# A decoder layer on one core: half of the last row's state sum moved to TensorE, the last x1 block kept on chip, the second norm by half rows

## What is computed

```
x1  = layernorm(x + attention(x))              # over the 4 rows at each position, causal, 16 heads of 32
u   = silu(conv4(in_proj(ctx)))                # 512 channels per row
h_t = exp(delta_t * A) * h_(t-1) + delta_t * u_t * B_t     # 16 states n per channel
y   = sum_n h[n] * C[n] + D * u
x2  = layernorm(x1 + y * silu(x1))             # "second norm"
out = layernorm(x2 + (silu(x2 Wg) * (x2 Wu)) Wd)
```

## Time and profile before

| | us |
|---|---|
| median of 3 runs | 1078.03 |
| lowest and highest | 1074.52, 1078.8 |
| the profiled execution: its own time | 1081.42 |
| the profiled execution: its span | 1079.6 |
| VectorE busy | 790.4 |
| TensorE busy | 856.6 |
| ScalarE, GpSimd busy | 697.5, 575.0 |

### The profile page before, as it was taken

The page is one execution under the profiler, slowest core; times in us unless marked ns, Lnnn a source line. Parts: engine busy times, 40 slices in busy tenths (PEclk is TensorE's granted clock), DMA queues, the critical chain, the costliest instruction groups (busy, mean ns, idle before and its releaser), DMA issues. The chain is left out here.

```text
span 1079.6 us, 12506 instructions
## 1 busy us (share of the span) xinstructions
PE 856.6 (79%) x3752; PEld 625.1 (58%) x3752; DVE 790.4 (73%) x1262; ACT 697.5 (65%) x1087; POOL 575.0 (53%) x561
## 2 busy tenths in 40 slices
PE   6868798687785978867652657779899999989997
PEld 2536654375443754455331445558777777778886
DVE  3587898877988679873872585699999999545543
ACT  3387995689757897584690464477777787333331
POOL 0049966897679976698695233145545455200000
PEclk8887877788887978888675787789999999999999
DMA  7146989689986898779799761111112111122321
GB/s 242 31 122 147 217 175 214 131 230 236 208 195 123 232 236 201 146 136 248 158 233 246 238 202 58 50 40 50 39 39 58 39 41 36 39 83 66 115 77 50
DMA packets 53686, 146.49 MB, mean 136 GB/s; under 512 B 5684, under 2 KB 14004, under 8 KB 43908
## 3 DMA queue, kind: packets, MB, share of 16 engines
q0 software_dynamic: 9216, 67.11, 32.5%
q1 hardware_dynamic: 43056, 78.53, 21.7%
q10 hardware_dynamic: 1364, 0.25, 0.1%
HBM read 58.97 MB, written 91.10 MB: 139 GB/s over the span
## 5 line engine op out<-in xcount | busy, mean ns | idle before, releaser
L1309 POOL TENSOR_TENSOR state<-state,crep 128x512 f32<-128x512 f32 x256 | 347.8, 1538 | 103.7 <-DVE state L1066 103.6
L1066 DVE TENSOR_TENSOR_SCAN state<-decay,banks 128x512 f32<-128x512 f32 x256 | 294.8, 1202 | 74.7 <-PE banks L566 49.6
L612 PE MATMUL banks<-x2T,wgu 128*128 128x512 f32 x1056 | 250.3, 399 | 28.8 <-POOL wgu L1401 27.3
L566 PE MATMUL banks<-ident,scaled 128*128 128x128 f32 x1024 | 182.1, 324 | 106.6 <-DVE state L1066 91.9
L612 PEld LDWEIGHTS banks<-x2T,wgu 128*128 128x128 f32 x1056 | 202.4, 193 | 75.7 <-issue 27.4
L566 PEld LDWEIGHTS banks<-ident,scaled 128*128 128x128 f32 x1024 | 139.0, 165 | 175.5 <-DVE state L1066 96.2
L788 ACT ACTIVATE decay<-delta,negA 128x512 f32<-128x512 f32 x256 | 170.8, 717 | 98.6 <-DVE state L1066 98.2
L777 ACT ACTIVATE scaled<-duT,BT 128x512 f32<-128x512 f32 x256 | 163.5, 716 | 9.9 <-DVE duT L1043 9.8
L892 ACT ACTIVATE leaf<-bit,table,table_gap 128x512 f32<-128x512 int32 x198 | 149.6, 806 | 20.4 <-DVE w L1095 20.4
L1095 DVE COPY_PREDICATED leaf<-bits,leaf 128x512 f32<-128x512 int32 x132 | 118.8, 914 | 8.0 <-issue 6.9
L1095 DVE COPY_PREDICATED w<-bits,leaf 128x512 f32<-128x512 int32 x99 | 90.1, 910 | 3.3 <-ACT leaf L892 1.7
(11 more groups left out here) (122 smaller groups left out, 1154.5 us busy)
## 6 DMA issues: line engine op xcount, KB each, us to landing
y_scratch<-state POOLq DMA_DIRECT2D x60, 1024.0 KB, 8.7
crep<-c_scratch SPq DMA_DIRECT2D x64, 256.0 KB, 5.3
idx_sb<-in_idx SPq DMA_DIRECT2D x33, 256.0 KB, 2.8
xT_sb<-in_xT SPq DMA_DIRECT2D x16, 256.0 KB, 4.6
x_sb<-in_x SPq DMA_DIRECT2D x4, 1024.0 KB, 19.0
y_scratch<-u SPq DMA_DIRECT2D x4, 1024.0 KB, 6.1
y_scratch<-state SPq DMA_DIRECT2D x4, 1024.0 KB, 6.1
x_scratch<-x_sb SPq DMA_DIRECT2D x4, 1024.0 KB, 8.8
```

Source lines behind the costliest of these rows:

```text
L566: last = nc.tensor.transpose(banks[:, k % NB, lc * LQ:(lc + 1) * LQ], scaled[:, g % SR, lc, et * P:(et + 1) * P], ident[:])
L612: last = mm(banks[:, 2 * tb + w, :], wgu[:, par, w, ws, t * P:(t + 1) * P], x2T[:, tb, xs, t, :], start=t == 0 and n == 0, stop=t == HT - ...
L1066: V.tensor_tensor_scan(state[:, g % GR, et, :], decay[:, k % DR_RING, :], banks[:, k % NB, :], 0.0, ALU.mult, ALU.add).then_inc(scan_ready, 1)
L1309: G.tensor_tensor(state[:, g % GR, et, :], state[:, g % GR, et, :], crep[:, g % CR, :], ALU.mult)\
```

## The change

1. For the last 8 of row 3's 16 states (`G0` = 56 of 64 groups) no DMA adds the products. TensorE adds them: one product with the identity for each unit (`state_summed`), three groups behind the transposes, into the four PSUM banks that are free after the projection; then y of the first eight states, loaded back, is added the same way (`rest_summed`), and `gate_y(3)` reads PSUM. `add_odd_sum(3)` moves up to (11, 3).
2. The last block's x goes into the buffer `conv_in` instead of `x_sb`, with its load moved from row 3's n = 5 to row 2's n = 13. Its x1 stays there and is neither stored nor loaded: `load_row` takes three quarters of x1, `x1_tile` takes the last quarter from the chip.
3. The row loads begin at n = 8 instead of 12. All four gates silu(x1) go to SBUF, in two instructions each. GpSimd multiplies rows 1 and 2 by them in one instruction each, VectorE row 0 in one and row 3 in four.
4. The second norm goes by eight half rows k, with two banks each, woven with parts of `select`.
5. The convolution taps of rows 1 to 3 move from (1, 0)...(1, 3) to (1, 2), (1, 3), (2, 0), (2, 1).

The core of the diff, with less indentation; where a function's body is new only its new lines are shown:

```diff
+sb("conv_at", [P, 72])
+conv_in = sb("conv_in", [P, ET, L])
...
+gate_in = ctx.enter_context(nc.sbuf_tensor("gate_in", [P, 2, ROW], f32))
...
+x_last = conv_in
+x_at = lambda c: x_sb if c < S - 1 else x_last
...
+G0 = DS * S - DS // 2
...
+    if g >= G0:
+        return ysum_out, ET * (g - G0) + ET
     if g % DS == 1:
...
+yb = [t[:, 0:ROW].rearrange("p (t l) -> p t l", l=L) for t in taken]
+x1b = [t[:, ROW:2 * ROW].rearrange("p (t h) -> p t h", h=H) for t in taken]
+gate = [gate_in[:, 0, :], gate_in[:, 1, :], gate_in[:, 0, :], flat_h[:, 2 * ROW:3 * ROW]]
+gate = [t.rearrange("p (t h) -> p t h", h=H) for t in gate]
+ON_POOL = {1: 1, 2: 2}
+GATED = {0: 1, 3: 5}
+row_gated = lambda b: (pool_gated, ON_POOL[b]) if b in ON_POOL else (gated, GATED[b])
+def x1_tile(b, lt):
+    return x1b[b][:, lt, :] if lt < 3 else x_last[:, b, :]
...
+HALVES = [(b, (2 * h, 2 * h + 1)) for b in range(S) for h in range(2)]
+def half_bank(k, i):
+    return 2 * (k % 4) + i
...
-            if c:
+            if c == S - 1:
+                sp.wait_ge(delta_ready, ET * S)
+                sp.wait_ge(x_in, 16 * c)
+            elif c:
                 sp.wait_ge(x1_out, 16 * c)
-            sp.dma_start(x_sb[:], x.rearrange("s (c p) h -> p s c h", p=P)[:, :, c, :]).then_inc(x_in, 16)
+            sp.dma_start(x_at(c)[:], x.rearrange("s (c p) h -> p s c h", p=P)[:, :, c, :]).then_inc(x_in, 16)
...
-            sp.dma_start(x1b[b], x1_scratch[b].rearrange("(t p) h -> p t h", p=P)).then_inc(x1_in[b], 16)
+            sp.dma_start(x1b[b][:, 0:3, :], x1_scratch[b].rearrange("(t p) h -> p t h", p=P)[:, 0:3, :])\
+                .then_inc(x1_in[b], 16)
             sp.dma_start(yb[b], y_scratch[b].rearrange("(p t) l -> p t l", p=P)).then_inc(y_in[b], 16)
...
-                if n == 5 and b:
+                if n == 5 and 0 < b < S - 1:
                     load_x(b)
+                if n == 13 and b == S - 2:
+                    load_x(b + 1)
...
-                if b == S - 1 and n == 10:
-                    store_x1(b)
-                if b == S - 1 and n == 12:
-                    sp.wait_ge(x1_out, 16 * S)
+                if b == S - 1 and n == 8:
+                    sp.wait_ge(shift_ready, S)
+                    sp.wait_ge(x1_out, 16 * (S - 1))
+                if b == S - 1 and 8 <= n < 8 + S - 1:
+                    load_row(n - 8)
+                if b == S - 1 and n == 11:
                     sp.dma_start(table[:], lut.to_broadcast([P, 16])).then_inc(lut_in, 16)
-                    load_idx(0, 0)
-                if b == S - 1 and n >= 12 and n - 12 < S - 1:
-                    load_row(n - 12)
-        load_idx(0, 1)
-        load_idx(0, 2)
+                    for c in range(3):
+                        load_idx(0, c)
+        sp.wait_ge(decay_ready, UNITS)
+        sp.wait_ge(scaled_ready, S * DS * S)
+        load_row(S - 1)
         store_x2(0)
         next_idx(0, 0)
-        load_row(S - 1)
         store_x2(1)
...
+        def state_summed(g, et):
+            if g == G0 and et == 0:
+                pe.wait_ge(res_ready, S * S)
+                pe.wait_ge(attT_ready, S * S)
+            pe.wait_ge(hc_ready, ET * g + et + 1)
+            mm(banks[:, NB + et, :], ident[:], state[:, g % GR, et, :], start=g == G0, stop=False)\
+                .then_inc(ysum_out, 1)
+        def rest_summed():
+            pe.wait_ge(y_in[S - 1], 16)
+            for et in range(ET):
+                mm(banks[:, NB + et, :], ident[:], yb[S - 1][:, et, :], start=False, stop=True)\
+                    .then_inc(ysum_out, 1)
         pe.wait_ge(ip_in, 16)
         pe.wait_ge(ident_in, 16)
...
+        def residual(k):
+            b, lts = HALVES[k]
+            if k < 2:
+                pe.wait_ge(scan_ready, UNITS)
+            elif k < 4:
+                pe.wait_ge(gated, GATED[S - 1])
+            else:
+                pe.wait_ge(x2lo_ready, 2 * (k - 4) + 2)
+            pe.wait_ge(*row_gated(b))
+            for i, lt in enumerate(lts):
+                if i + k == 0:
+                    pe.wait_ge(x1_ready, S * S)
+                mm(banks[:, half_bank(k, i), :], ident[:], x1_tile(b, lt), start=True, stop=False)
                 for et in range(4):
...
-        residual(1, range(4))
-        x2_over(0)
-        residual(2, range(4))
-        x2_over(1)
+        residual(0)
+        residual(1)
+        for k in range(6):
+            residual(k + 2)
+            x2_over(k)
         gate_up(0, 0, (0,), first=True)
-        x2_over(2)
+        x2_over(6)
         gate_up(0, 0, (1,), first=True)
-        residual(3, (0, 1))
-        gate_up(0, 0, (2,), first=True)
-        residual(3, (2, 3))
-        x2_over(3)
-        gate_up(0, 0, (3,), first=True)
+        x2_over(7)
+        gate_up(0, 0, (2, 3), first=True)
         with pe.Fori(1, FT - 1, 2) as f:
...
         def gates(b):
             act.wait_ge(x1_in[b], 16)
...
+            act.wait_ge(x1_ready, S * S)
+            if b == 2:
+                act.wait_ge(gated, GATED[0])
+            elif b == 3:
+                act.wait_ge(dbu_out, UNITS)
+            A(gate[b][:, 0:3, :], x1b[b][:, 0:3, :], ACT.Silu).then_inc(gate_ready, 1)
...
+        def x2T_hi(k):
+            b, h = divmod(k, 2)
+            if k == 0:
+                act.wait_ge(*row_gated(2))
+            elif h == 0:
                 act.wait_ge(x2_out[b - 1], 16)
+            for j in range(2):
+                act.wait_ge(x2T_out, 2 * k + j + 1)
+                A(x2T[:, b, 0, 2 * j:2 * j + 2, h * 2 * P:(h + 1) * 2 * P],
+                  banks[:, half_bank(k, j), :].rearrange("p (t n) -> p t n", t=2), ACT.Copy)\
+                    .then_inc(x2hi_ready, 1)
...
         act.wait_ge(gap_ready, 1)
         leaves(0, 0, 0, early, first=True)
         norm_apply(0)
         leaves(0, 0, 0, late, first=True)
+        norm_apply(1)
         x2T_hi(0)
-        gates(2)
         leaves(0, 1, 0, early, first=True)
-        norm_apply(1)
+        norm_apply(2)
+        x2T_hi(1)
         leaves(0, 1, 0, late, first=True)
-        x2T_hi(1)
+        norm_apply(3)
+        x2T_hi(2)
         leaves(0, 2, 0, early, first=True)
-        norm_apply(2)
-        x2T_hi(2)
-        leaves(0, 2, 0, late, first=True)
-        gates(3)
-        leaves(1, 0, 1, early)
-        norm_apply(3)
-        leaves(1, 0, 1, late)
         norm_apply(4)
         x2T_hi(3)
+        norm_apply(5)
+        x2T_hi(4)
+        leaves(0, 2, 0, late, first=True)
+        norm_apply(6)
+        x2T_hi(5)
+        norm_apply(7)
+        x2T_hi(6)
+        x2T_hi(7)
+        leaves(1, 0, 1)
...
         def gate_y(b):
+            dve.wait_ge(gate_ready, {0: 2, 3: 6}[b])
             dve.wait_ge(y_in[b], 16)
+            if b == S - 1:
+                for et in range(ET):
+                    dve.wait_ge(ysum_out, ET * (DS * S - G0) + et + 1)
+                    V.tensor_tensor(yb[b][:, et, :], banks[:, NB + et, :], gate[b][:, et, :], ALU.mult)\
+                        .then_inc(gated, 1)
+            else:
+                V.tensor_tensor(yb[b], yb[b], gate[b], ALU.mult).then_inc(gated, 1)
...
+                V.tensor_tensor(x2T[:, b, 1, 2 * j:2 * j + 2, h * 2 * P:(h + 1) * 2 * P],
+                                banks[:, half_bank(k, j), :].rearrange("p (t n) -> p t n", t=2),
+                                x2T[:, b, 0, 2 * j:2 * j + 2, h * 2 * P:(h + 1) * 2 * P].bitcast(f32),
+                                ALU.subtract).then_inc(x2lo_ready, 1)
         def inner(f, tb):
...
+        TAPS_AT = {(1, 2): 0, (1, 3): 1, (2, 0): 2, (2, 1): 3}
...
-                            earlier_taps(m, et)
+                        if at in TAPS_AT:
+                            earlier_taps(m, TAPS_AT[at])
...
-                    if not more and at == (15, 1):
-                        gate_y(0)
-        norm_stats(0)
-        gate_y(1)
         dve.wait_ge(lut_in, 16)
         pairs = table[:].rearrange("p (j two) -> p j two", two=2)
         V.tensor_tensor(table_gap[:], pairs[:, :, 1], pairs[:, :, 0], ALU.subtract).then_inc(gap_ready, 1)
         for k in range(3):
             take_bit(k, 0, 0, 0)
-        norm_shift(0)
-        select(0, 0, 0)
-        x2T_lo(0)
-        norm_stats(1)
-        gate_y(2)
-        norm_shift(1)
-        select(0, 1, 0)
-        x2T_lo(1)
-        norm_stats(2)
-        norm_shift(2)
-        x2T_lo(2)
-        select(0, 2, 0)
-        norm_stats(3)
-        norm_shift(3)
+        for b in (0, 3):
+            gate_y(b)
+        MUXES = [((0, 0), (0, 1, 2)), ((0, 0), (3, 4, 5)), ((0, 0), (6,)), ((0, 1), (0, 1, 2)),
+                 ((0, 1), (3, 4, 5, 6)), ((0, 2), (0, 1)), ((0, 2), (2, 3)), ((0, 2), (4, 5, 6))]
+        for k in range(2 * S):
+            norm_stats(k)
+            (f, c), steps = MUXES[k]
+            select(f, c, f, steps)
+            norm_shift(k)
+            if k >= 2:
+                x2T_lo(k - 2)
+        x2T_lo(6)
+        x2T_lo(7)
         select(1, 0, 1)
-        norm_stats(4)
-        norm_shift(4)
```

(31 more changed lines are left out.)

140 lines of the change are left out of this document (54 added, 86 removed).

## The result

The changed kernel takes 1026.25 us (median of four runs, 1022.06 to 1027.44). The kernel before took 1078.41 us beside it. The ratio is 0.9514, with a 95% interval of 0.9474 to 0.9553. The time lies inside the range of the prediction, 998 to 1042, and 8.6 us above its 1017.7. The profiled execution has a span of 1025.4 us, against 1079.6 before: 54.2 us less, where 60.3 were forecast. In the medians it is 52.2 us less; the kernel before was profiled in one of its longer executions.

The account below looks back on a forecast made before the run. VectorE and DMA were taken as near their limit in rows 1 and 2, the transition as a chain between engines, VectorE full afterwards. Gains 25.6 + 25.3 + 9.4 = 60.3 us gave 1021 profiled, 1017.7 median; range 998 to 1042.

Parts of the forecast that it names:

- rival E: Feed-forward loop: select(1, 1, 1) starts earlier but the loop takes as much longer; 1078 us, chance 0.02.
- The signs named at the end of the prediction: Profile marks; wrong if pairs at 2 us, last-row additions over 15 us after issue, or transition rstd waits over 20.
- The x load: Last row: VectorE's 14.41 us wait for x goes, 2.2 us for TensorE comes; scan (7, 1) at 517.8.
- The taps: Rows 0 to 2: VectorE's waits for first taps go, 9.4 us for three rows; ends 0 and 13.
- The end of the scans: Last row: GpSimd's products end at 570 us, TensorE free at 574.6, residual(0) 25.6 us earlier.
- rival D: TensorE stays at the low clock with its sums; 66 us of loss, 1084 us, chance 0.03.
- The transition: From residual(0) to select(1, 1, 1): 50.6 us VectorE work plus 21.3 waits, 72 instead of 97.3; gain 25.3.
- Rival A: DMA engines hold the last row, additions and row loads in each other's way; 1038 us, chance 0.28 with B.
- Rival B: Transition: half rows don't shorten the chain, 2.5 us more for each of eight; 1038 us, chance 0.28 with A.
- Rival C: Transition takes 55 us instead of 72, near VectorE's own 50.6, taps give 13; 997 us, chance 0.17.
- The 2.4 us that the prediction named: Shared port: gate_y(0), with both inputs in SBUF, would hold up GpSimd's products once, making the sum 2.4 us worse.

Follow-up runs that it names:

- the taps alone: Kernel before with only the convolution taps put two scans later; 1074.75 us, ratio 0.9983.
- The pair with half additions: Kernel before with additions in HBM moving only half the columns, without and with moved taps; 1046.96 and 1034.97 us, ratios 0.9722 and 0.9609.
- whole rows: Changed kernel with the second norm's eight half rows taken two by two on all engines; 1036.36 us, ratio 0.9653.
- sums of half the positions: Changed kernel with TensorE's sums after the first group over 256 of 512 positions; 1023.99 us, ratio 0.9528.
- ten groups: Changed kernel with ten groups' states summed on TensorE instead of eight, two groups behind the transposes; 1019.54 us, ratio 0.9466.
- the combinations: Changed kernel with sums two behind and gates on VectorE, 1020.91 us; ten groups, two behind, 1019.54; all three, 1016.98.
- the second run of the changed kernel itself: Changed kernel without further edits, timed again beside three combinations on one chip; 1023.09 us, ratio 0.9499.

## Why the prediction was right, and where it was off

*The mechanism was right.* Both waits of the earlier trace rows went, the gain arrived at the end to within 0.4 us (rival E is out), and the forecast was off by 6.1 us of 60.3. That it was so near is in part luck: two terms were too high by 5.3 and 6.3 us, and one too low by 5.1. The signs named at the end of the prediction show it too. GpSimd's last product ended at 565.2 us for 561, the first `residual` started at 576.8 for 565, and `select(1, 1, 1)` at 643.8 for 637; the pairs ran at 1.02 us and the wait for x was gone, but the first taps still waited, 1.32 us. One sign of being wrong could not tell anything: two additions of the last row landed 15.6 us after their issue, over the 15 named, but in the kernel before the same two had taken 16.6.

*The x load.* (7, 1) was forecast at 517.8, which with the 4.1 us of the earlier rows is 513.7; it started at 513.52. Loading x late again costs 13.9 us where 12.2 were forecast.

*The taps, 9.4 forecast and 4.1 measured.* The step that failed is "at the limit none of it would stay ... I take 9.4, as row 0 has no wait for DMA and the others keep 0.12 of slack". The waits for the taps did not go whole, but shrank by 2.2 us each. Row 0 kept 3.5 us (from its first scan to its last but one 131.2 us in the kernel before, 127.7 in the changed one); the other half microsecond lies ahead of it. Rows 1 and 2 added nothing: 133.1 us each time for row 1, 130.9 and 130.8 for row 2 up to the last row's scans. With the taps alone, row 1's scans were some 4.3 us ahead by what row 1 itself had gained; 2.7 of them went in the longer wait for an addition (4.93 us for 2.22), and the rest before 281 us, where VectorE has a new wait of 1.44 us for TensorE. The pair with half additions shows that it is the additions that decide: 12.0 us against 1.8 in the times, 10.2 against 4.2 at the last row. A mean share of 0.88 did not leave 0.12 of slack at the one place where a scan needed its addition.

*The end of the scans, 25.6 forecast and 19.3 measured.* GpSimd's last product ended at 565.2, forecast 570 less 4.1. (34 products of 1.23 us from 526.5 end at 568.3, not at 569; this changes little.) The pairs ran at 1.02 us from 545.38 on, 1.30 us for a unit with its sum, as the sum had 0.43 + 0.86; only the first ones took 1.92 at the lower clock, so rival D is out. What failed is "After the last product at 570 one sum": three groups' sums and one more (13) stood behind the last transpose, at 0.86 us each, 11.2 us from 562.4. The order in the queue was in the diff, and I had counted it as if TensorE could follow each product. Two groups behind instead of three gives 3 to 5 of these 6.3 us back at `residual`, though in the time nothing that can be told. The wait at (11, 0), for which I had put 1 us, took 6.73. It is 6.04 with two groups behind, and is not there with two additions fewer. It costs less than its length: GpSimd, which still had products to make, stood idle for only 1.34 us (before 539.51) and ended when forecast.

*The transition, 25.3 forecast and 30.4 measured.* VectorE's own work was forecast at 50.6 us and is 50.67. The waits were forecast at 21.3 and are 16.3. Those with a name held: 3.36 us for the rstd at 595.98 (forecast 3.9), 4.98 for `x2_over(7)` (5.4). Not there were the 2.8 us for the first rstd: I had GpSimd's second multiplication in front of it, but that was over at 579.26, before the variance at 581.5, as `residual(0)` came 6.3 us later than I thought. So what TensorE's queue lost was in part given back here; when the queue is shortened, the price appears in the rows (the variance of 1.92 us). The leaves of the next tile cost 1.3 us (0.61 and 0.65), not 3.

*Rival A* (the DMA engines hold the last row): half right in its mechanism, at 6.73 us of one wait, and not in its size. The DMA share fell from 0.91 to 0.80. *Rival B* (half rows bring nothing): out, as they bring 10.8 us. The 97.3 us that I gave the transition without them was too much: with whole rows it takes 76.5 us up to the first inner tile, and in the kernel before it took 95.6, so most of the gain was to be had without them. *Rival C*: 16.3 us of waits remained instead of near 4.

*The two engines that exclude each other.* `gate_y(0)` did not hold up a product, as it ran after the last one. It held GpSimd's bits behind them: 3.44 us at 570.29 where they take 1.5 elsewhere in this trace, off the path. The Trainium skill (SBUF — State Buffer, Who interferes with whom) says that a VectorE instruction with two inputs in SBUF and a GpSimd one that reads SBUF block each other for the whole instruction. The trace agrees that each holds up the other, as above and below; but VectorE was held for longer than one instruction, as the last section shows. The 2.4 us that the prediction named (2.28 here) fell where nothing waits for them. The larger price came from the other direction, and I had not put it into the sum: GpSimd's stream holds VectorE's small instructions until it pauses (6.14 us for two tiles of bits at 564.03, where they take 1.16 with two groups behind; 9.01 and 10.84 for `table_gap` in variants). In the changed kernel it is covered by TensorE's 13 sums; once these are gone it is the next bound, as sums of half the positions and ten groups both show.

*Left open.* Which part of the 19.0 us of the transition is the clock, and which the data that stand ready; and whether `table_gap`, moved ahead of the scans, would give the combinations their missing microseconds. Neither was tried.

## What to carry to other kernels

When work is moved into the queue of another engine, count what stands behind its last dependent instruction in the order that the code gives, not what is left to do when the data arrive: here 13 sums stood there, 11.2 us, where one had been counted. A gain upstream of transfers that others wait for may be lost even where the DMA engines' mean share is below one, as here at 0.88; test it by making the transfers smaller, and see in which stage the time then goes. After removing one wait, look for the small instruction behind it: it is hidden as long as something larger is late.

## What the runs showed of the hardware that was not expected

A VectorE instruction on 128x8 elements with both inputs in SBUF (`table_gap`), queued beside GpSimd's back-to-back products of 1.2 us, took 1.86 to 10.84 us in nine of the ten profiles with the changed order, 7.31 in the second run of the changed kernel itself. It did not slip in between two products, but ended, to within 0.1 us, when GpSimd's stream paused (568.39 and 568.36; 566.12 and 566.08). Not each time: in the first profile of the changed kernel it took 0.18 us at 563.59, within the same stream, and the bits after it 6.14. What decides between the two is open. The scans of the same VectorE, with one input in PSUM, ran beside the same products at 1.2 us each (42.09 us for 35).

The bytes of the additions were worth more outside of the waits for additions than in them. With half of them the kernel before went from 1076.8 to 1046.96 us, with its scans, products and transposes unchanged. VectorE's waits for additions in rows 1 and 2, 1 to 2.3 us each and 9.0 in all, can't give that. The waits for two loads in the last row can: the one for x shrank from 14.41 to 4.96 us, the one for y from 17.57 to 2.06.
